# A gated cross-attention kernel on one core: part of the second attention's exponentials moved from ScalarE to VectorE

## Chip, cores and metric

The kernel runs on one core of one Trainium2 chip. The metric is the device time of one execution in microseconds. The engines are called as the profile calls them: PE is TensorE's matmul queue and PEld its weight loads, ACT is ScalarE, DVE is VectorE, POOL is GpSimd, SP is SyncE.

## What is computed

The reference runs two gated blocks over 1024 text rows of width 128 and 6404 context rows of width 96: a first cross-attention (4 heads, top 32 keys) with its own feed-forward part, a low-rank feed-forward block, the second cross-attention, and a mixture of 8 experts. Only the second cross-attention matters here. It has 16 heads of width 8 and a full softmax over all 6404 keys:

```
q = (x @ wq + bq);  k = (y @ wk + bk);  v = (y @ wv + bv)      # 16 heads of 8
scores = einsum('bhqd,bhkd->bhqk', q, k) / sqrt(8)
attn = softmax(scores);  out = einsum('bhqk,bhkd->bhqd', attn, v) @ wo + bo
```

That is 16 x 1024 x 6404 exponentials, 105 million.

## The kernel before

The program is a chain of stages with a barrier after each. The stage of lines 1833 to 1947 is the second attention. Keys lie on the partitions of a score tile and queries on its columns: a tile is 128 keys by 512 queries of one head in f32, which is one PSUM bank. The work goes in 8 passes (`NPASS`): 4 quads of heads by 2 halves of the queries. In a pass the 6404 keys are 50 whole blocks of 128 (`FULL1`) and one last block, whose four heads share one tile on 32 partitions each (`LEFT`). So a pass has 4 x 50 + 1 = 201 tiles (`NTILE`), taken three at a time: 67 units (`NU`).

For each unit PE makes three score matmuls (line 1890, bf16, 52 rows of the contraction, so that two heads lie on the two halves of the array's rows) into three of six PSUM banks, two sets of three in turn. ACT takes the exponential of the three banks in one ACTIVATE of 1536 columns (line 1936) into the ring `ex1` of 12 slots, that is 4 units. PE then sums the values: for a block of keys whose four tiles are done, four f32 matmuls of the weights V (9 columns: 8 values and a one for the sum) into one bank, side by side on four column tiles (line 1905; the trace counts each as two instructions, so a group is 8; line 1909 is the last block's). The exponentials carry no maximum: a bound on the scores, tested in the stage before against `EXP_RANGE`, selects a general path only where it is needed.

The order on PE is written out: `scores(w, u)`, then the group of values that became ready two units back (`ready_at`). Two waits set the pace:

```
pe.wait_ge(S("exped1"), w * NU + u - 1)        # scores(u): the exponentials of unit u-2 are done
act.wait_ge(S("scored1"), w * NU + u + 1)      # ACT: the scores of unit u are done
```

DVE does nothing in a pass but copy the four sums from PSUM at its end (line 1946). POOL clears `o1` once at the start of the stage (line 1862). SP loads the keys and values of quads 2 and 3 as the two buffers come free (line 1866).

Of the kernel before, what the change touches and what calls it, by code (L numbers as in the profile page):

```python
# [25 lines left out]
NG = -(-G // P)  # L26
# [4 lines left out]
H1, DH1 = 16, 8  # L31
VW = DH1 + 1
# [7 lines left out]
NPIECE = G // PIECE  # L40
MASKED = -1.0e30
LOWEST = -3.0e38
EXP_RANGE = 60.0
LN_EPS = 1e-5
ROUND = 12582912.0
assert GP == NG * P
# [46 lines left out]
def program(nc, A, whole):  # L93
# [3 lines left out]
    def S(name):  # L97

        if name not in stage_sems:
            stage_sems[name] = nc.alloc_semaphore(name=f"{name}_{stage[0]}")  # L100
        return stage_sems[name]
# [22 lines left out]
    ps = whole.enter_context(nc.psum_tensor("ps", [P, 8, 512], F32))  # L124
# [1165 lines left out]
    FULL1 = G // P  # L1290
    LEFT = 32
# [4 lines left out]
    K1 = sb(k1s, "K1", [P, 2, 2, GP], BF16)  # L1296
    V1 = sb(k1s, "V1", [P, 2, NG, 4 * VW])

    ROWS1 = ROW1 + LEVELS + 1
# [236 lines left out]
    Q1 = sb(q1s, "Q1", [P, H1, T], BF16)  # L1536
# [71 lines left out]
    with ExitStack() as b7:  # L1608
# [8 lines left out]
        qsel = sb(b7, "qsel", [P, 2, LEVELS, P], BF16)  # L1617
        qline = sb(b7, "qline", [P, 1])
        QP = 3
        SC1 = float(DH1) ** -0.5  # L1620
        with nc.Block() as block:
            @block.sync
            def _(sp):
# [56 lines left out]
            def _(act):  # L1680
# [12 lines left out]
                act.wait_ge(S("bq1s"), 1)  # L1693
                C.activation(qs[:, :], flat(ps[:, 2:4, :]), ACT.Identity, bias=bq1s[:, 0:1], scale=SC1).then_inc(S("q1_sb"), 1)
                act.wait_ge(S("qline_in"), 16)
# [7 lines left out]
            def _(dve):  # L1703
                w = lambda t: t[:, :, :]
                V.tensor_scalar(bq1s[:, :], bq1[:, :], SC1, None, ALU.mult).then_inc(S("bq1s"), 1)
                dchain(V.tensor_scalar(b2r[:, :], b2r[:, :], gt[:, 2:3], None, ALU.mult))
# [24 lines left out]
                dchain(V.reduce_max(bound1[:, :], boundh[:, :], AX.X))  # L1731
                dchain(V.tensor_scalar(bound1[:, :], bound1[:, :], EXP_RANGE, None, ALU.is_gt))
                dchain(V.tensor_copy(general[0:1, 1:2], bound1[:, :]))
# [97 lines left out]


    with ExitStack() as b8:
        NSLOT, NBANK = 12, 3
        ex1 = sb(b8, "ex1", [P, NSLOT, TB])
        NPASS = NQ * NB
        NTILE = 4 * FULL1 + 1
        NU = NTILE // NBANK
        assert NTILE % NBANK == 0 and NSLOT % NBANK == 0


        def last_tile(g):
            return min(4 * g + 3, NTILE - 1)

        def ready_at(g):
            return last_tile(g) // NBANK + 2

        def group_of(tile):

            w, n = divmod(tile, NTILE)  # L1850
            return w * NG + min(n // 4, FULL1)

        def bank(w, n):
            return (w * NTILE + n) % (2 * NBANK)

        def slot(w, n):
            return (w * NTILE + n) % NSLOT

        with nc.Block() as block:
            @block.gpsimd  # L1860
            def _(pool):
                PL.memset(o1[:, :, :], 0.0).then_inc(S("o1_zero"), 1)

            @block.sync
            def _(sp):
                for quad in range(2, NQ):

                    sp.wait_ge(S("scored1"), (quad - 1) * NB * NU)
                    sp.wait_ge(S("summed1"), (quad - 1) * NB * NG)
                    load_quad(sp, quad, S(f"k1_in{quad % 2}"), S(f"v1_in{quad % 2}"))  # L1870

            @block.tensor
            def _(pe):
                def scores(w, u):
                    quad, tb = divmod(w, NB)
                    if quad >= 2 and tb == 0 and u == 0:
                        pe.wait_ge(S(f"k1_in{quad % 2}"), 16 * KIN * (quad // 2))
                    if w * NU + u >= 2:
                        pe.wait_ge(S("exped1"), w * NU + u - 1)
                    for n in range(NBANK * u, NBANK * u + NBANK):  # L1880
                        g = n // 4
                        for hh in ([n % 4] if g < FULL1 else range(4)):
                            rows_ = slice(64 * (hh % 2), 64 * (hh % 2) + ROWS1)
                            if g < FULL1:
                                out, col = ps[:, bank(w, n), :], 0
                                keys = slice(g * P, (g + 1) * P)
                            else:
                                out, col = ps[LEFT * hh:LEFT * (hh + 1), bank(w, n), :], LEFT * hh
                                keys = slice(g * P, g * P + LEFT)
                            last = M.matmul(out, K1[rows_, quad % 2, hh // 2, keys],  # L1890
                                            Q1[rows_, 4 * quad + hh, tb * TB:(tb + 1) * TB], start=True, stop=True,
                                            tile_position=(64 * (hh % 2), col))
                    last.then_inc(S("scored1"), 1)

                def values(w, g):
                    quad = w // NB
                    if g == 0:
                        if quad >= 2 and w % NB == 0:
                            pe.wait_ge(S(f"v1_in{quad % 2}"), 16 * VIN * (quad // 2))
                        if w >= 2:  # L1900
                            pe.wait_ge(S("o1_read"), 4 * (w - 1))
                    for j in range(4):
                        out = ps[32 * j:32 * j + VW, 6 + w % 2, :]
                        if g < FULL1:
                            last = M.matmul(out, V1[:, quad % 2, g, VW * j:VW * j + VW], ex1[:, slot(w, 4 * g + j), :],  # L1905
                                            start=g == 0, stop=False, tile_position=(0, 32 * j))
                        else:
                            left = slice(LEFT * j, LEFT * (j + 1))
                            last = M.matmul(out, V1[left, quad % 2, g, 0:VW], ex1[left, slot(w, NTILE - 1), :],  # L1909
                                            start=False, stop=True, tile_position=(LEFT * j, 32 * j))  # L1910
                    last.then_inc(S("summed1"), 1)

                for w in range(NPASS):
                    for u in range(NU):
                        scores(w, u)
                        for g in range(NG):
                            if w and ready_at(g) == NU + u:
                                values(w - 1, g)
                        for g in range(NG):
                            if ready_at(g) == u:  # L1920
                                values(w, g)
                for g in range(NG):
                    if ready_at(g) >= NU:
                        pe.wait_ge(S("exped1"), (NPASS - 1) * NU + ready_at(g) - 1)
                        values(NPASS - 1, g)

            @block.scalar
            def _(act):
                for w in range(NPASS):
                    for u in range(NU):  # L1930
                        act.wait_ge(S("scored1"), w * NU + u + 1)
                        over = w * NTILE + NBANK * u + NBANK - 1 - NSLOT
                        if over >= 0:
                            act.wait_ge(S("summed1"), group_of(over) + 1)
                        s, b = slot(w, NBANK * u), bank(w, NBANK * u)
                        C.activation(ex1[:, s:s + NBANK, :], ps[:, b:b + NBANK, :], ACT.Exp)\  # L1936
                            .then_inc(S("exped1"), 1)

            @block.vector
            def _(dve):  # L1940
                dve.wait_ge(S("o1_zero"), 1)
                for w in range(NPASS):
                    quad, tb = divmod(w, NB)
                    dve.wait_ge(S("summed1"), (w + 1) * NG)
                    for j in range(4):
                        V.tensor_copy(o1[32 * j:32 * j + VW, quad, tb * TB:(tb + 1) * TB],  # L1946
                                      ps[32 * j:32 * j + VW, 6 + w % 2, :]).then_inc(S("o1_read"), 1)

    q1s.close()
    k1s.close()  # L1950
# [270 lines left out]
```

## Time and profile before

| | us |
|---|---|
| median of 3 runs | 1854.99 |
| lowest, highest | 1853.83, 1858.27 |
| the profiled execution's own time | 1853.31 |
| its span, first to last instruction | 1851.5 |
| the second attention, first score to last copy | 932.2 to 1666.4 |

The rows come from one profiled execution. Times of the timeline and of windows are microseconds from the start of the span. A group of instructions shows its busy time, the mean of one in ns, and the idle time of its engine just before it, with what ended most of it. Instructions of one engine overlap: the mean of one can be longer than the step from one to the next.

### The profile page before, as it was taken

The page shows a single profiled execution, that of the slowest core. Times are in us where ns is not written, and L with a number is a line of the kernel's source. Part 1 is how long each engine was busy: PE and PEld are TensorE (multiplying, and loading weights), DVE is VectorE, ACT ScalarE, POOL GpSimd, SP SyncE. Part 2 cuts the span into 40 slices and gives each one's busy share as a digit, 9 for nine tenths or more (in the row PEclk, how much of TensorE's full clock was granted, in tenths as well). Part 3 has the DMA queues.
Part 4 walks back from the last instruction along what each step waited for, and adds up shares of the span by engine and source line. Part 5 has one row for each costly group of instructions (what it writes and reads, how often), then busy time and mean ns, then how long its engine had stood idle before and what let it go on. Part 6 is the DMA issues. An engine that isn't in the chain of part 4 may idle for free. (4 is left out here: it accounts for less than half of the span.)

```text
span 1851.5 us, 22757 instructions
## 1 busy us (share of the span) xinstructions
PE 1582.9 (85%) x8261; PEld 603.4 (33%) x8261; DVE 854.8 (46%) x2331; ACT 1373.1 (74%) x1441; POOL 169.9 (9%) x154
## 2 busy tenths in 40 slices
PE   6789788898998993776789999999999999985996
PEld 4463354554554552533211111111111111113442
DVE  7768999999999997473400000000000000003223
ACT  5737687888887874313289999999999999982332
POOL 4840211111111101000000000000000000000000
PEclk8869899999999996787689999999999999997998
DMA  3430968979769679350000004000500000003000
GB/s 103 144 117 0 184 150 177 202 155 210 174 151 230 152 179 241 78 152 7 18 1 1 1 1 63 13 1 1 75 1 1 1 1 1 1 1 98 0 1 12
DMA packets 69263, 143.41 MB, mean 77 GB/s; under 512 B 21993, under 2 KB 40642, under 8 KB 68218
## 3 DMA queue, kind: packets, MB, share of 16 engines
q0 software_dynamic: 13616, 75.73, 20.5%
q1 hardware_dynamic: 55098, 65.30, 13.2%
q8 instruction: 69, 1.13, 0.2%
q10 hardware_dynamic: 432, 0.85, 0.1%
q14 instruction: 48, 0.39, 0.1%
HBM read 52.65 MB, written 13.99 MB: 36 GB/s over the span
## 5 line engine op out<-in xcount | busy, mean ns | idle before, releaser
L1936 ACT ACTIVATE ex<-ps 128x1536 f32<-128x1536 f32 x536 | 721.9, 1494 | 6.0 <-PE ps L1890 6.0
L1905 PE MATMUL ps<-ex,V 128*9 128x512 f32 x3200 | 419.8, 597 | 0.5 <-ACT ex L1936 0.4
L850 PE MATMUL ps<-K,qst 128*128 128x512 f32 (+1 forms) x832 | 392.9, 604 | 30.7 <-ACT srow L920 20.7
L1890 PE MATMUL ps<-Q,K 52*128 52x512 bf16 (+1 forms) x1632 | 322.8, 385 | 39.1 <-ACT ex L1936 34.2
L1946 DVE COPY o<-ps 9x512 f32<-9x512 f32 x32 | 22.0, 687 | 714.2 <-PE ps L1909 713.5
L1051 DVE MAX8 cand<-srow 128x8 f32<-128x200 f32 (+1 forms) x1024 | 318.7, 359 | 8.7 <-ACT srow L920 8.6
L1011 DVE SCALAR_TENSOR_TENSOR both<-srow,top,both 128x1536 f32<-128x1536 f32 (+1 forms) x128 | 239.4, 1870 | 21.2 <-ACT both L937 21.0
L920 ACT COPY srow<-ps 128x1024 f32<-128x1024 f32 (+1 forms) x224 | 205.1, 924 | 46.1 <-PE ps L850 45.7
L937 ACT ACTIVATE both<-srow,shift 128x1536 f32<-128x1536 f32 (+1 forms) x128 | 209.4, 1638 | 23.2 <-DMA both<-both 21.8
L1890 PEld LDWEIGHTS ps<-Q,K 52*128 52x128 bf16 (+1 forms) x1632 | 60.7, 94 | 448.1 <-ACT ex L1936 433.1
L850 PEld LDWEIGHTS ps<-K,qst 128*128 128x128 f32 x832 | 150.8, 198 | 166.5 <-issue 116.1
L884 PE MATMUL ps<-v_ring,meanT 128*128 128x128 f32 x716 | 106.1, 293 | 55.3 <-DMA v_ring<-v_rows 49.7
L884 PEld LDWEIGHTS ps<-v_ring,meanT 128*128 128x128 f32 x716 | 95.8, 202 | 97.0 <-issue 48.4
L1103 POOL DMA_DIRECT2D both<-both x92 | 79.1, 860 | 520.1 <-DVE both L1011 486.3
L1905 PEld LDWEIGHTS ps<-ex,V 128*9 128x9 f32 x3200 | 47.7, 89 | 171.2 <-issue 169.4
L2119 ACT ACTIVATE hidm<-ps,b1m 128x512 f32<-128x512 f32 x64 | 43.4, 688 | 75.4 <-PE ps L2072 75.3
L866 PE MATMUL ps<-ident,both 128*128 128x128 f32 (+1 forms) x408 | 64.6, 284 | 17.7 <-DVE both L1071 7.2
L2155 DVE TENSOR_TENSOR hidp<-hidm,ps 128x2048 f32<-128x2048 f32 x16 | 36.6, 2288 | 90.2 <-PE ps L2080 82.3
L866 PEld LDWEIGHTS ps<-ident,both 128*128 128x128 f32 (+1 forms) x408 | 52.0, 146 | 66.4 <-issue 62.2
L2072 PE MATMUL ps<-wT,w1m 128*128 128x512 f32 x128 | 60.2, 615 | 1.4 <-ACT hidm L2119 0.9
L962 ACT COPY meanT<-ps 128x512 f32<-128x512 f32 x96 | 55.9, 585 | 7.1 <-PE ps L866 7.1
L2097 PE MATMUL ps<-hidp,w2m 128*128 128x512 f32 x128 | 58.9, 605 | 0.0
(333 smaller groups left out, 1087.2 us busy)
## 6 DMA issues: line engine op xcount, KB each, us to landing
both<-both POOLq DMA_DIRECT2D x69, 768.0 KB, 8.9
v_ring<-v_rows SPq DMA_DIRECT2D x84, 256.0 KB, 6.3
both<-both POOLq DMA_DIRECT2D x23, 898.0 KB, 13.1
K<-k_parts SPq DMA_DIRECT2D x48, 204.0 KB
k_parts<-kl SPq DMA_DIRECT2D x12, 384.0 KB, 2.6
V<-v_rows SPq DMA_DIRECT2D x4, 900.0 KB, 6.7
v_rows<-v1g SPq DMA_DIRECT2D x12, 288.0 KB, 3.8
srow<-v_rows SPq DMA_DIRECT2D x1, 3200.0 KB, 17.5
```

The source lines that it names most:

```text
L850: last = M.matmul(ps[:, BANK_OF[item] + b, 0:c1 - c0], qst[:, h, :], K0[:, c0:c1], start=True, stop=True)
L866: last = M.transpose(ps[0:w, turn_bank(m), (c % 4) * P:(c % 4 + 1) * P], both[:, mean_of(u), c * P:c * P + w], ident[:, :])
L884: last = M.matmul(ps[:, 7, 0:D], meanT[0:w, m % MSLOTS, (c % 4) * P:(c % 4 + 1) * P], v0_tile(u, c)[0:w, :], start=c == 0, stop=c == NG - 1)
L920: C.copy(srow[:, n % SLOTS, g0:g1], ps[:, b:b + -(-(g1 - g0) // 512), :].rearrange("p a b -> p (a b)")[:, 0:g1 - g0])\
L937: C.activation(both[:, home(n), chunk(c)], srow[:, s, chunk(c)], ACT.Exp, bias=shift[:, s:s + 1])\
L1011: V.scalar_tensor_tensor(both[:, home(n), chunk(c)], srow[:, s, chunk(c)], top40[:, s, TOPK - 1:TOPK], both[:, home(n), chunk(c)], ALU.is_ ...
L1051: last = V.max(eight, srow[:, n % SLOTS, c0:c1])
L1103: PL.dma_start(both[:, mean_of(t), c0:c0 + step], both[:, 0, c0:c0 + step], accum_op=ALU.add).then_inc(S(f"added{c}"), 16)
L1890: last = M.matmul(out, K1[rows_, quad % 2, hh // 2, keys], Q1[rows_, 4 * quad + hh, tb * TB:(tb + 1) * TB], start=True, stop=True, tile_po ...
L1905: last = M.matmul(out, V1[:, quad % 2, g, VW * j:VW * j + VW], ex1[:, slot(w, 4 * g + j), :], start=g == 0, stop=False, tile_position=(0, ...
L1936: C.activation(ex1[:, s:s + NBANK, :], ps[:, b:b + NBANK, :], ACT.Exp)\
L2072: M.matmul(ps[:, f, :], w1[:, e, f * P:(f + 1) * P], wT[:, tb * TB:(tb + 1) * TB], start=True, stop=True).then_inc(S("hidm_ps"), 1)
```

## The change

Three whole key blocks of each pass (47, 48 and 49) leave the units: 4 x 47 + 1 = 189 tiles stay with ACT. Their 12 tiles per pass go to every fifth unit from the seventh on (`OWN` is 6, 11, ..., 61): such a unit has two tiles for ACT and, in its third bank, one of the moved tiles. The number of units stays 67. ACT's instruction for such a unit has 1024 columns, that of the others 1536.

DVE takes the exponential of a moved tile in nine chained instructions on 128 x 512 (`power_of_two`): it reads the bank with a lower bound, rounds the score to a whole number by adding a large constant, forms the fraction, evaluates a polynomial of degree 4 in Horner's form, shifts the rounded number's bits into an exponent, and multiplies. The polynomial is monic, without its leading coefficient `LEAD`, so DVE's exponentials are too large by 1/`LEAD`; ACT gives its own the same factor by the bias `log(1/LEAD)`, a column `common` that POOL sets in the stage's start. The scores are now in units of log 2 (the factor `LOG2E` goes into the scale of the queries), and ACT multiplies by `LN2` in its instruction.

PE sums a block of the moved tiles (`own_values`) when four are done, five units after the last of them (`LATE_AT`: units 26, 46 and 66), from the ring `power` of 8 tiles. Before a unit's scores PE also waits until DVE has read the moved tile of the unit that used the bank (`own_read`). The ring `ex1` is now addressed by units. DVE copies a pass's sums (`read_sums`) ahead of the next pass's tiles. The core of the diff:

```diff
-EXP_RANGE = 60.0
+LOG2E = float(np.log2(np.e))
+LN2 = float(np.log(2.0))
+EXP_RANGE = 60.0 * LOG2E
...
-        SC1 = float(DH1) ** -0.5
+        SC1 = float(DH1) ** -0.5 * LOG2E
...
+        BATCH, BATCHES, EVERY, FIRST_U = 4, 3, 5, 6
+        NOWN = BATCH * BATCHES
+        OWN = [FIRST_U + EVERY * i for i in range(NOWN)]
+        REGULAR = FULL1 - BATCHES
...
+                PL.memset(common[:, :], float(np.log(1.0 / LEAD))).then_inc(S("common_ready"), 1)
...
                     if w * NU + u >= 2:
                         pe.wait_ge(S("exped1"), w * NU + u - 1)
+                        if own_before(w * NU + u - 1):
+                            pe.wait_ge(S("own_read"), own_before(w * NU + u - 1))
...
+                    if u in OWN:
+                        b, j = divmod(OWN.index(u), BATCH)
+                        last = score_tile(w, ps[:, bank(w, u, NBANK - 1), :], 0, REGULAR + b, j)
...
+                def own_values(w, b):
+
+                    quad = w // NB
+                    pe.wait_ge(S("powered"), w * NOWN + BATCH * (b + 1))
+                    for j in range(BATCH):
+                        last = M.matmul(ps[32 * j:32 * j + VW, 6 + w % 2, :], V1[:, quad % 2, REGULAR + b, VW * j:VW * j + VW],
+                                        power[:, (w * NOWN + BATCH * b + j) % (2 * BATCH), :], start=False, stop=False,
+                                        tile_position=(0, 32 * j))
+                    last.then_inc(S("power_used"), 1)
...
+                        if u in LATE_AT:
+                            own_values(w, LATE_AT[u])
...
+                act.wait_ge(S("common_ready"), 1)
                 for w in range(NPASS):
                     for u in range(NU):
                         act.wait_ge(S("scored1"), w * NU + u + 1)
...
-                        C.activation(ex1[:, s:s + NBANK, :], ps[:, b:b + NBANK, :], ACT.Exp)\
+                        s, b, n = slot(w, u, 0), bank(w, u, 0), len(UNITS[u])
+                        C.activation(ex1[:, s:s + n, :], ps[:, b:b + n, :], ACT.Exp, scale=LN2, bias=common[:, 0:1])\
                             .then_inc(S("exped1"), 1)
...
+                def power_of_two(w, i):
+
+                    m = w * NOWN + i
+                    if m:
+                        dve.wait_ge(S("powered"), m)
+                    dve.wait_ge(S("scored1"), w * NU + OWN[i] + 1)
+                    V.tensor_scalar(score[:, :], ps[:, bank(w, OWN[i], NBANK - 1), :], LOW2, None, ALU.max)\
+                        .then_inc(S("own_read"), 1)
+                    dve.wait_ge(S("own_read"), m + 1)
+                    dchain(V.tensor_scalar(whole_[:, :], score[:, :], ROUND2, None, ALU.add))
+                    dchain(V.scalar_tensor_tensor(part[:, :], whole_[:, :], ROUND2, score[:, :], ALU.subtract, ALU.subtract))
+                    dchain(V.scalar_tensor_tensor(poly[:, :], part[:, :], POWER[4], part[:, :], ALU.add, ALU.mult))
+                    for k in (3, 2, 1):
+                        dchain(V.scalar_tensor_tensor(poly[:, :], poly[:, :], POWER[k], part[:, :], ALU.add, ALU.mult))
+                    bits = whole_[:, :].bitcast(I32)
+                    dchain(V.tensor_scalar(bits, bits, 23, None, ALU.logical_shift_left))
+                    if m // BATCH >= 2:
+                        dve.wait_ge(S("power_used"), m // BATCH - 1)
+                    V.scalar_tensor_tensor(power[:, m % (2 * BATCH), :], poly[:, :], POWER[0], whole_[:, :], ALU.add, ALU.mult)\
+                        .then_inc(S("powered"), 1)
```

## Rows read from the trace of the kernel before

**Rows 1.** The page's engine line: busy us, share of the span, instructions.
```profile
PE 1582.9 (85%) x8261; PEld 603.4 (33%) x8261; DVE 854.8 (46%) x2331; ACT 1373.1 (74%) x1441; POOL 169.9 (9%) x154
```

**Rows 2.** Windows: length, then busy PE, PEld, DVE, ACT, POOL; granted clock; DMA share; GB/s.
```profile
942.00:1660.00 718.00, 684.67 (x4839) 107.89 (x4838) 19.24 (x28) 713.54 (x531) 0.00 (x0) 1.00 0.07 11
```

**Rows 3.** The page's groups: busy us, mean ns of one | idle before, releaser.
```profile
L1936 ACT ACTIVATE ex<-ps 128x1536 f32<-128x1536 f32 x536 | 721.9, 1494 | 6.0 <-PE ps L1890 6.0
L1890 PE MATMUL ps<-Q,K 52*128 52x512 bf16 (+1 forms) x1632 | 322.8, 385 | 39.1 <-ACT ex L1936 34.2
L1946 DVE COPY o<-ps 9x512 f32<-9x512 f32 x32 | 22.0, 687 | 714.2 <-PE ps L1909 713.5
```

**Rows 4.** Timeline of ACT: start us, us, engine, line, operation.
```profile
1409.71 31.04 ACT L1936 ACTIVATE ex<-ps 128x1536 f32<-128x1536 f32 x23
```

**Rows 5.** Timeline of PE in the fifth pass.
```profile
1320.82 0.60 PE L1890 MATMUL ps<-Q,K 52*128 52x512 bf16 x3
1321.36 1.04 PE L1905 MATMUL ps<-ex,V 128*9 128x512 f32 x8
1322.34 0.60 PE L1890 MATMUL ps<-Q,K 52*128 52x512 bf16 x3
```

**Rows 6.** Timeline of PE and ACT at a pass's first units.
```profile
1300.88 0.82 PE L1890 MATMUL ps<-Q,K 52*128 52x512 bf16 x6
1301.52 9.51 ACT L1936 ACTIVATE ex<-ps 128x1536 f32<-128x1536 f32 x7 [0.65 <-PE ps L1890]
```

**Rows 7.** Lines and timeline of ACT, from PSUM, no bias column (ns min/median/max).
```profile
L403 ACT ACTIVATE Q<-ps x1: 1023/1023/1023, 16.8 to 16.8; 128x1024 f32<-128x1024 f32 x1
...
407.49 1.93 ACT L920 COPY srow<-ps 128x1024 f32<-128x1024 f32 x2
...
L920 ACT COPY srow<-ps x39: 356/1012/1045, 400.8 to 499.9; 128x1024 f32<-128x1024 f32 x33, 128x260 f32<-128x260 f32 x6
```

**Rows 8.** Lines and timeline of ACT, from PSUM, with a bias column.
```profile
L1699 ACT ACTIVATE Q<-ps,qline x8: 1095/1108/1109, 915.4 to 928.0; 64x1024 bf16<-64x1024 f32 x8
...
917.86 2.11 ACT L1699 ACTIVATE Q<-ps,qline 64x1024 bf16<-64x1024 f32 x2 [1.39 <-PE ps L1670]
...
1706.77 3.00 ACT L2119 ACTIVATE hidm<-ps,b1m 128x512 f32<-128x512 f32 x5
...
L2119 ACT ACTIVATE hidm<-ps,b1m x64: 680/687/712, 1706.8 to 1824.9; 128x512 f32<-128x512 f32 x64
```

**Rows 9.** Timeline and lines of DVE, one and two tensors; POOL beside them.
```profile
14.11 0.23 DVE L489 SCALAR_TENSOR_TENSOR q<-z,q 128x64 f32<-128x64 f32 x1
14.37 0.20 DVE L453 TENSOR_SCALAR q<-q 128x64 f32<-128x64 f32 x1
...
L1507 DVE TENSOR_TENSOR sum_x<-spec_x x2: 682/687/692, 796.0 to 801.6; 128x512 f32<-128x512 f32 x2
...
L1717 DVE CAST ql<-qs x1: 687/687/687, 910.2 to 910.2; 128x1024 bf16<-128x1024 f32 x1
...
L452 DVE TENSOR_TENSOR phase<-rowsT,steps 128x4096 f32<-128x4096 f32 x1 | 4.4, 4416 | 0.0
...
58.97 5.26 DVE L466 SCALAR_TENSOR_TENSOR phaseA<-ub,phaseA 128x4096 f32<-128x4096 f32 x1
...
60.01 4.69 POOL L361 CAST kl<-res 128x512 bf16<-128x512 f32 x1
```

**Rows 10.** Timeline of ACT and POOL at the stage's start and earlier.
```profile
932.23 1.28 ACT L1936 ACT_TABLE_LOAD   x1 [3.07 <-PEq L106]
932.23 3.50 POOL L1862 MEMSET o<- 128x4096 f32 x1 [65.53 <-POOLq L106]
933.52 5.48 ACT L1936 ACTIVATE ex<-ps 128x1536 f32<-128x1536 f32 x4
...
0.27 0.10 POOL L2207 MEMSET const-float32-1.0<- 128x1 f32 x1
...
48.40 1.28 ACT L380 ACT_TABLE_LOAD   x1 [0.34 <-DVE phase L466]
```

More of the change, by code:

```diff
@@ L1833, in program @@
     with ExitStack() as b8:
-        NSLOT, NBANK = 12, 3
-        ex1 = sb(b8, "ex1", [P, NSLOT, TB])
-        NPASS = NQ * NB
[L1837 to L1857, printed above, removed]
+        NBANK, NHELD = 3, 4
+        BATCH, BATCHES, EVERY, FIRST_U = 4, 3, 5, 6
+        NOWN = BATCH * BATCHES
+        OWN = [FIRST_U + EVERY * i for i in range(NOWN)]
+        REGULAR = FULL1 - BATCHES
+        NPASS = NQ * NB
+        NTILE = 4 * REGULAR + 1
+        NSUM = REGULAR + 1
+        ex1 = sb(b8, "ex1", [P, NHELD * NBANK, TB])
+        power = sb(b8, "power", [P, 2 * BATCH, TB])
@@ new lines, in program @@
+        score, whole_, part = (sb(b8, name, [P, TB]) for name in ("score", "whole_part", "part"))
+        poly = score
+        common = sb(b8, "common", [P, 1])
+        UNITS, at = [], 0
+        while at < NTILE:
+            n = NBANK - 1 if len(UNITS) in OWN else NBANK
+            UNITS.append(list(range(at, at + n)))
+            at += n
+        NU = len(UNITS)
+        assert at == NTILE and max(OWN) + EVERY < NU
+        PLACE = {tile: (u, n) for u, tiles in enumerate(UNITS) for n, tile in enumerate(tiles)}
@@ new lines, in program, with block_of @@
+        LATE_AT = {OWN[BATCH * (b + 1) - 1] + EVERY: b for b in range(BATCHES)}
+        LAST_OF = [min(4 * g + 3, NTILE - 1) for g in range(NSUM)]
+        READY_AT = [PLACE[tile][0] + 2 for tile in LAST_OF]
+        LOW2, ROUND2 = -118.0, ROUND + 127.0 + 256.0
+        LEAD = 0.0013276471518916786
+        POWER = tuple(c / -LEAD for c in (1.0000000716546564, -0.6931469670638629, 0.2402211972393386, -0.055507132749627305,
+                                          0.009675541330686871))
+        def block_of(g):
+            return g if g < REGULAR else FULL1
@@ L1859, in program, with own_before, bank, slot @@
+        def own_before(k):
+            w, u = divmod(k, NU)
+            return w * NOWN + sum(1 for o in OWN if o < u)
+        def bank(w, u, n):
+            return (w * NU + u) % 2 * NBANK + n
+        def slot(w, u, n):
+            return (w * NU + u) % NHELD * NBANK + n
         with nc.Block() as block:
@@ L1868, in _ @@
                     sp.wait_ge(S("scored1"), (quad - 1) * NB * NU)
-                    sp.wait_ge(S("summed1"), (quad - 1) * NB * NG)
+                    sp.wait_ge(S("summed1"), (quad - 1) * NB * NSUM)
                     load_quad(sp, quad, S(f"k1_in{quad % 2}"), S(f"v1_in{quad % 2}"))
@@ L1873, in _, with score_tile @@
             def _(pe):
+                def score_tile(w, out, col, g, hh):
+                    quad, tb = divmod(w, NB)
+                    rows_ = slice(64 * (hh % 2), 64 * (hh % 2) + ROWS1)
+                    keys = slice(g * P, (g + 1) * P) if g < FULL1 else slice(g * P, g * P + LEFT)
+                    return M.matmul(out, K1[rows_, quad % 2, hh // 2, keys], Q1[rows_, 4 * quad + hh, tb * TB:(tb + 1) * TB],
+                                    start=True, stop=True, tile_position=(64 * (hh % 2), col))
                 def scores(w, u):
@@ L1879, in scores @@
                         pe.wait_ge(S("exped1"), w * NU + u - 1)
[L1880 to L1892, printed above, removed]
+                        if own_before(w * NU + u - 1):
+                            pe.wait_ge(S("own_read"), own_before(w * NU + u - 1))
+                    for n, tile in enumerate(UNITS[u]):
+                        g, j = block_of(tile // 4), tile % 4
+                        if g < FULL1:
+                            last = score_tile(w, ps[:, bank(w, u, n), :], 0, g, j)
+                        else:
+                            for hh in range(4):
+                                last = score_tile(w, ps[LEFT * hh:LEFT * (hh + 1), bank(w, u, n), :], LEFT * hh, g, hh)
+                    if u in OWN:
+                        b, j = divmod(OWN.index(u), BATCH)
+                        last = score_tile(w, ps[:, bank(w, u, NBANK - 1), :], 0, REGULAR + b, j)
                     last.then_inc(S("scored1"), 1)
@@ L1903, in values @@
                         out = ps[32 * j:32 * j + VW, 6 + w % 2, :]
-                        if g < FULL1:
-                            last = M.matmul(out, V1[:, quad % 2, g, VW * j:VW * j + VW], ex1[:, slot(w, 4 * g + j), :],
+                        if g < REGULAR:
+                            last = M.matmul(out, V1[:, quad % 2, g, VW * j:VW * j + VW], ex1[:, slot(w, *PLACE[4 * g + j]), :],
                                             start=g == 0, stop=False, tile_position=(0, 32 * j))
@@ L1908, in values @@
                             left = slice(LEFT * j, LEFT * (j + 1))
-                            last = M.matmul(out, V1[left, quad % 2, g, 0:VW], ex1[left, slot(w, NTILE - 1), :],
+                            last = M.matmul(out, V1[left, quad % 2, FULL1, 0:VW], ex1[left, slot(w, *PLACE[NTILE - 1]), :],
                                             start=False, stop=True, tile_position=(LEFT * j, 32 * j))
                     last.then_inc(S("summed1"), 1)
+                def own_values(w, b):
[6 more added lines that the diff above has]
+                    last.then_inc(S("power_used"), 1)
                 for w in range(NPASS):
@@ L1915, in _ @@
                         scores(w, u)
-                        for g in range(NG):
-                            if w and ready_at(g) == NU + u:
+                        for g in range(NSUM):
+                            if w and READY_AT[g] == NU + u:
                                 values(w - 1, g)
-                        for g in range(NG):
-                            if ready_at(g) == u:
+                        for g in range(NSUM):
+                            if READY_AT[g] == u:
                                 values(w, g)
-                for g in range(NG):
-                    if ready_at(g) >= NU:
-                        pe.wait_ge(S("exped1"), (NPASS - 1) * NU + ready_at(g) - 1)
+                        if u in LATE_AT:
+                            own_values(w, LATE_AT[u])
+                for g in range(NSUM):
+                    if READY_AT[g] >= NU:
+                        pe.wait_ge(S("exped1"), (NPASS - 1) * NU + READY_AT[g] - 1)
                         values(NPASS - 1, g)
@@ L1931, in _ @@
                         act.wait_ge(S("scored1"), w * NU + u + 1)
[L1932 to L1935, printed above, removed]
-                        C.activation(ex1[:, s:s + NBANK, :], ps[:, b:b + NBANK, :], ACT.Exp)\
+                        if w * NU + u >= NHELD:
+                            ow, ou = divmod(w * NU + u - NHELD, NU)
+                            act.wait_ge(S("summed1"), ow * NSUM + UNITS[ou][-1] // 4 + 1)
+                        s, b, n = slot(w, u, 0), bank(w, u, 0), len(UNITS[u])
+                        C.activation(ex1[:, s:s + n, :], ps[:, b:b + n, :], ACT.Exp, scale=LN2, bias=common[:, 0:1])\
                             .then_inc(S("exped1"), 1)
@@ L1940, in _, with read_sums @@
             def _(dve):
-                dve.wait_ge(S("o1_zero"), 1)
-                for w in range(NPASS):
+                def read_sums(w):
                     quad, tb = divmod(w, NB)
-                    dve.wait_ge(S("summed1"), (w + 1) * NG)
+                    dve.wait_ge(S("power_used"), (w + 1) * BATCHES)
+                    dve.wait_ge(S("summed1"), (w + 1) * NSUM)
                     for j in range(4):
@@ L1947, in _ @@
                                       ps[32 * j:32 * j + VW, 6 + w % 2, :]).then_inc(S("o1_read"), 1)
+                def power_of_two(w, i):
[17 more added lines that the diff above has]
+                        .then_inc(S("powered"), 1)
+                dve.wait_ge(S("o1_zero"), 1)
+                for w in range(NPASS):
+                    if w:
+                        read_sums(w - 1)
+                    for i in range(NOWN):
+                        power_of_two(w, i)
+                read_sums(NPASS - 1)
     q1s.close()
```

## The prediction

> **What bounds the kernel now.** I read the page's engine line first: PE is busy for 85% of the span and ACT for 74% [rows 1], so no engine bounds the whole, and the stage has to be read by itself. The second view is the stretch from 942 to 1660 us, the second attention: in 718 us ACT is busy for 713.54, PE for 684.67, DVE for 19.24, and PE's granted clock is 1.00, the upper of its two levels, 2.4 GHz [rows 2]. Then the groups of instructions: 536 ACTIVATEs of line 1936 sat idle for only 6.0 us in all, while PE sat idle 39.1 us in front of its scores, 34.2 of it for those ACTIVATEs, and DVE waited 714 us [rows 3]. So ACT ends last and PE is about 5% behind it: whatever is taken from ACT is paid out only until PE is full.
>
> The pace comes from the timeline. 23 ACTIVATEs take 31.04 us, and the last of them 1.494, so one follows another after (31.04 − 1.494)/22 = 1.343 us [rows 3, 4]; 536 of them are 719.8 us. On PE the three score matmuls of a unit hold the queue for 0.54 us and a group of values for 0.98 [rows 5], so a unit with a group costs 1.51 against ACT's 1.343, and a unit without one 0.54. Per pass PE needs 67 × 0.54 + 51 × 0.98 = 86.2 us, ACT 90.0. From the start of a unit's scores to its ACTIVATE takes 0.64 us where ACT waits [rows 6].
>
> **Part 1: ACT's elements.** 12 units of 67 in each pass go from 1536 to 1024 columns. Two copies of 1024 columns from PSUM take 1.93 us, one lasts 1.012, so their pace is 0.92 [rows 7]; against 1.343 that is 0.42 us less per unit, for 8 × 12 = 96 units −40.6 us.
>
> **Part 2: ACT's bias.** All 536 ACTIVATEs get the column `common` as bias, where line 1936 has none. The trace has both kinds from PSUM at 1024 columns: without a bias column 1.023 us [rows 7], with one 1.108 [rows 8], so 0.085 more. That it isn't hidden under the neighbour is seen from two paces with a bias: two in 2.11 us give 2.11 − 1.108 = 1.00, against 0.92 without; and five of 512 columns in 3.00 us give (3.00 − 0.69)/4 = 0.578 [rows 8], to which 1024 columns at (1.343 − 0.92)/512 each add 0.846: 1.424 for 1536. I take 1.343 + 0.085 = 1.428 for three banks and 1.00 for two. No row shows an Exp from PSUM with a bias, so the ends are 0 (hidden, the first rival) and 0.13: an Exp of 1536 columns lasts 1.494, which is 0.05 more than 1.023 and 512 more columns give, and that much may come on top; I take 0.085, which two rows give independently. Price: 536 × 0.085 = +45.6 us.
>
> The Trainium skill has a rule that speaks against this change ("ScalarE: Activation LUTs", section "What ACT_TABLE_LOAD costs"): each per-partition pointer operand adds about 93 ns to an ACTIVATE, whatever the function, and back-to-back ones overlap by about 93. By its figure the price would be an estimated 49.8 us in place of 45.6. The trace agrees on the price within 10%; on the overlap it differs, since 1.494 less 1.343 is 0.151 here [rows 3, 4], and the measurement decides.
>
> Parts 1 and 2 together: 440 × 1.428 + 96 × 1.00 = 724.3 us, +4.5 against 719.8. The bias costs more than the three key blocks save.
>
> **Part 3: PE between the ACTIVATEs.** Its matmuls stay the same in number (47 + 3 + 1 groups, 201 tiles per pass). But a unit's scores may not start before the ACTIVATE two units earlier has ended, and ACT must have them 0.64 us before its own start. With the new paces PE may be late by 2 × 1.428 − 1.58 − 0.64 = 0.64 us. Around units 26 and 46, where a group of values from DVE's tiles falls on a unit that has none of its own, five units in a row carry a group: PE loses 4 × 0.08, and 1.51 − 1.00 = 0.51 at the short unit, 0.83 in all, and ACT waits about 0.2. With some hundredths at other short units this is 0.4 us per pass: +3.5 us, 0 to 8. The wait for `own_read` that now stands in front of the scores is met long before: the copy ends 0.7 us after the scores, and the unit that needs the bank is two units on.
>
> **Part 4: the nine DVE instructions.** Per tile: one from PSUM (0.69, as the 512-column copies of line 1946 [rows 3]); two on SBUF with a constant, the addition and the shift; six scalar_tensor_tensor. These take 0.23 at 64 columns, and an instruction with two tensors of 512 columns takes 0.687 [rows 9], so 0.69 each. An SBUF instruction with one tensor has 0.20 at 64 and 0.687 at 1024 columns, so some 0.43 at 512 [rows 9]; for the shift of integers no row exists, and it lies between 0.43 and 0.69. The step from one chained instruction to the next costs 14.37 − 14.11 − 0.23, about 0.03 [rows 9]. Sum: 0.69 + 2 × 0.43 + 6 × 0.69 + 9 × 0.03 = 6.0 us, 6.3 with a slow shift. The upper end is a scalar_tensor_tensor that ran for 5.26 us where a two-tensor instruction of its shape took 4.416 [rows 9], a factor of 1.19, while POOL worked beside it [rows 9]: 6.8 to 7.1 us. A period of five units is 4 × 1.428 + 1.00 = 6.71 us. So I cost it at nothing: it lies in DVE's idle 714 us [rows 3], as do the four copies of `read_sums`, which are due four units ahead of the first tile. If that cover goes, PE stands in `own_values` at `powered`, with the next scores queued behind, and ACT behind those.
>
> **Part 5: the first ACTIVATE.** ACT now waits for `common`, which POOL sets behind its memset of `o1`: 932.23 + 3.50 and 0.1 to 0.2 for the small one, 935.9 [rows 10]. The first ACTIVATE started at 933.52, behind a table load of 1.28 that ran from 932.23 [rows 10]. Delay 2.4 us if the load still runs ahead of the wait, 3.7 if behind it. At line 380, where two waits stand ahead of one ACTIVATE, the load came at 48.40, when the awaited work was done [rows 10]; so I take +3.7.
>
> **Sum:** +4.5 + 3.5 + 3.7 = +11.7 us. The profiled execution took 1853.31 us (span 1851.5), which gives 1865.0; the median of the runs, 1854.99, lies 1.7 higher, and I state **1867**.
>
> **Rival 1: the bias is hidden (not slower).** The column could be fetched while the ACTIVATE in front is still at work, which overlaps the next by 0.151 us anyway. Place: the seam between ACTIVATEs. ACT then needs 440 × 1.343 + 96 × 0.92 = 679.2 us, and PE's 8 × 86.2 = 690 would be the bound. Carrying the start rule of part 3 through ten units by hand gives waits of ACT of 0.22 per five units and in all some 4.5 per pass in place of 0.8: 679.2 + 36 = 715 against 719.8 + 6.0, −11, and with part 5 −7: 1848. It decides once the bias costs under 0.04 us each. For it: no row is an Exp from PSUM with a bias. Against it: two separate paces with a bias, Identity and Gelu, which both give 1.42 to 1.43 [rows 8]. Chance 0.13.
>
> **Rival 2: DVE's chain is too long.** If it exceeds 6.7 us, lateness adds up from tile to tile: a pass then takes 11 chains and 12 units, 11c + 17.1 + 0.7 us for a chain of c; for c = 7.0 that is 94.8 × 8 = 758 against 726, +32, and with part 5 1891; for 6.8 about 1873. For it: the factor of 1.19 above. Against it: that one ran beside POOL, which does nothing in this stage [rows 2]. Chance 0.11.
>
> **Rival 3: half of the bias is hidden,** between 0.03 and 0.06 us each: waits and savings nearly cancel, −6 to +2, with part 5 1853 to 1860. Chance 0.10.
>
> The forecast keeps 0.66: 1860 to 1877, from the ends of parts 3 and 5 and a bias of 0.075 to 0.10.
>
> **Numbers.** About 0.3%, 5.6 us, is what a measurement of this kernel can tell from no change: bounds 1849.4 and 1860.6. Faster has most of rival 1, 0.10; the same has rival 3, the rest of rival 1 and the lower edge of the forecast, 0.18; slower 0.72. The range 1848 to 1884 leaves out half of rival 1 and the worse half of rival 2.
>
> **What would show it.** Right: ACTIVATEs of line 1936's successor at about 1.58 us with 23 in some 32 to 33 us, short ones following after 1.00; ACT idle of 8 to 12 us, PE's idle for ACT up from 34 to about 45; nine DVE instructions in 6.0 to 6.3; first ACTIVATE at about 937. Part 2 is wrong if three banks still follow at 1.34; then ACT's idle rises to some 35 us and PE is the bound. Part 4 is wrong if PE waits for DVE's `power`.

## The result, and the profile after

The changed kernel takes 1867.38 us (median of 6 executions) against 1854.99 before; the ratio is 1.0064, 95% interval 1.0045 to 1.0083, so it is slower, by 0.6%. One of its six executions took 5131.85 us; the ratio leaves it out, no profile of it exists, and the median of the other five is 1866.12. The profiled execution has a span of 1866.8 us.

The spans alone mislead a little: the second attention begins at 935.64 us in this profile and at 932.23 before, and in the profiles further down at 929.2 to 942.6, though the kernels differ ahead of it in constants alone. So I compare the stage by itself, from POOL's memset of `o1` to the end of the last copy of the sums: 734.15 us before (932.23 [rows 10] to 1663.54 + 2.84), 746.29 after (935.64 to 1679.09 + 2.84), 12.1 us more.

The page's groups of the changed kernel, which answer to [rows 3] (busy us, mean ns of one | idle before, releaser), and the groups of ACT with the forms kept apart:

```profile
L1982 ACT ACTIVATE ex<-ps,common 128x1536 f32<-128x1536 f32 (+1 forms) x536 | 731.1, 1483 | 7.7 <-PE ps L1905 6.5
L1905 PE MATMUL ps<-Q,K 52*128 52x512 bf16 (+1 forms) x1632 | 322.7, 385 | 51.4 <-ACT ex L1982 45.1
L2002 DVE TENSOR_SCALAR score<-ps 128x512 f32<-128x512 f32 x96 | 66.4, 692 | 105.6 <-PE ps L1905 105.6
...
L1982 ACT ACTIVATE ex<-ps,common 128x1536 f32<-128x1536 f32 x440 | 647.7, 1558 | 7.7 <-PE ps L1905 6.5 <-POOL common L1888 1.2
L1982 ACT ACTIVATE ex<-ps,common 128x1024 f32<-128x1024 f32 x96 | 109.3, 1139 | 0.0
```

ACT exponentiates 96 tiles fewer and is nevertheless busy for 9.2 us more, 731.1 against 721.9. PE waits more for it, 45.1 us against 34.2. DVE's tiles wait for PE 105.6 us in all, so DVE is not what ends last.

The pace stands in ACT's timeline of the changed kernel; the four lines are the same run of ACTIVATEs, cut after its sixth, seventh, eighth and ninth instruction (start us, us):

```profile
1407.13 8.27 ACT L1982 ACTIVATE ex<-ps,common 128x1536 f32<-128x1536 f32 x6
...
1407.13 9.70 ACT L1982 ACTIVATE ex<-ps,common 128x1536 f32<-128x1536 f32 x7
...
1407.13 10.71 ACT L1982 ACTIVATE ex<-ps,common 128x1536 f32<-128x1536 f32 x8
...
1407.13 12.14 ACT L1982 ACTIVATE ex<-ps,common 128x1536 f32<-128x1536 f32 x9
```

The eighth is a short one, of 1024 columns. Long ones end 1.43 us apart (9.70 − 8.27). The short one starts 1.43 after the seventh and lasts 1.14; the ninth ends at 12.14 and lasts 1.56, so it starts 1.01 after the short one. The paces are 1.43 and 1.01 us, against 1.343 for every unit before [rows 4].

One whole pass, from unit 2 to unit 2 of the next, on ACT's timeline, first of the kernel before, then of the changed one:

```profile
1029.15 90.19 ACT L1936 ACTIVATE ex<-ps 128x1536 f32<-128x1536 f32 x67 [0.57 <-PE ps L1890]
1119.91 5.48 ACT L1936 ACTIVATE ex<-ps 128x1536 f32<-128x1536 f32 x4 [0.57 <-PE ps L1890]
```

```profile
1036.02 91.36 ACT L1982 ACTIVATE ex<-ps,common 128x1536 f32<-128x1536 f32 x67 [0.71 <-PE ps L1905]
1128.09 2.97 ACT L1982 ACTIVATE ex<-ps,common 128x1536 f32<-128x1536 f32 x2 [0.71 <-PE ps L1905]
```

A pass takes 92.07 us in place of 90.76, 1.31 more. The paces account for 55 × 1.43 + 12 × 1.01 − 67 × 1.343 = 0.79 of it. The other 0.52 is put down to waiting between ACTIVATEs, by subtraction: most of it is too short to be listed, since one ACTIVATE still counts as busy while the next could start.

One chain of DVE, the stage's windows and the stage's start in the changed kernel (timeline of DVE; windows with the columns of [rows 2]; timeline of POOL and ACT):

```profile
1409.60 0.69 DVE L2002 TENSOR_SCALAR score<-ps 128x512 f32<-128x512 f32 x1 [2.92 <-PE ps L1905]
1410.32 0.43 DVE L2005 TENSOR_SCALAR whole_part<-score 128x512 f32<-128x512 f32 x1
1410.78 0.69 DVE L2006 SCALAR_TENSOR_TENSOR part<-whole_part,score 128x512 f32<-128x512 f32 x1
...
1412.24 2.15 DVE L2009 SCALAR_TENSOR_TENSOR score<-score,part 128x512 f32<-128x512 f32 x3
1414.42 0.43 DVE L2011 TENSOR_SCALAR whole_part<-whole_part 128x512 int32<-128x512 int32 x1
1414.88 0.69 DVE L2014 SCALAR_TENSOR_TENSOR power<-score,whole_part 128x512 f32<-128x512 f32 x1
1416.25 0.69 DVE L2002 TENSOR_SCALAR score<-ps 128x512 f32<-128x512 f32 x1 [0.68 <-PE ps L1905]
```

```profile
942.00:1660.00 718.00, 675.73 (x4759) 105.38 (x4763) 554.40 (x874) 711.46 (x523) 0.00 (x0) 1.00 0.07 11
```

```profile
935.64 3.50 POOL L1887 MEMSET o<- 128x4096 f32 x1 [66.49 <-POOLq L108]
936.77 1.28 ACT L1982 ACT_TABLE_LOAD   x1 [4.20 <-PE ps L1905]
939.09 0.09 POOL L1888 MEMSET common<- 128x1 f32 x1
939.22 5.83 ACT L1982 ACTIVATE ex<-ps,common 128x1536 f32<-128x1536 f32 x4 [1.17 <-POOL common L1888]
```

A chain runs from 1409.60 to 1415.57, 5.97 us, and DVE then waits 0.68 for its next tile. DVE goes from 19 to 554 us busy in the stretch without being waited for. The granted clock is 1.00 as before. The first ACTIVATE comes 3.58 us after the stage's start, against 1.29 before [rows 10].

### The profile page after: what moved, and what is told of

Its sections match the earlier page's. It is cut to its first block and busy times, and to the rows that moved or that the text cites. A ratio compares the mean times of both kernels' runs of the same rounds, so it can differ in the third digit from the quotient of the medians.

```text
span 1866.8 us, 24340 instructions
## 1 busy us (share of the span) xinstructions
PE 1586.0 (85%) x8261; PEld 605.4 (32%) x8261; DVE 1405.2 (75%) x3195; ACT 1382.5 (74%) x1441; POOL 160.8 (9%) x155
## 5 line engine op out<-in xcount | busy, mean ns | idle before, releaser
L1982 ACT ACTIVATE ex<-ps,common 128x1536 f32<-128x1536 f32 (+1 forms) x536 | 731.1, 1483 | 7.7 <-PE ps L1905 6.5
L1938 PE MATMUL ps<-ex,V 128*9 128x512 f32 x3008 | 394.6, 597 | 0.2 <-ACT ex L1982 0.2
L1905 PE MATMUL ps<-Q,K 52*128 52x512 bf16 (+1 forms) x1632 | 322.7, 385 | 51.4 <-ACT ex L1982 45.1
L2009 DVE SCALAR_TENSOR_TENSOR score<-score,part 128x512 f32<-128x512 f32 x288 | 199.4, 692 | 9.8
L2002 DVE TENSOR_SCALAR score<-ps 128x512 f32<-128x512 f32 x96 | 66.4, 692 | 105.6 <-PE ps L1905 105.6
L2006 DVE SCALAR_TENSOR_TENSOR part<-whole_part,score 128x512 f32<-128x512 f32 x96 | 66.5, 693 | 3.3
L2014 DVE SCALAR_TENSOR_TENSOR power<-score,whole_part 128x512 f32<-128x512 f32 x96 | 66.4, 692 | 3.3
```

The costliest lines, as they stand in the source:

```text
L1905: return M.matmul(out, K1[rows_, quad % 2, hh // 2, keys], Q1[rows_, 4 * quad + hh, tb * TB:(tb + 1) * TB], start=True, stop=True, tile_po ...
L1982: C.activation(ex1[:, s:s + n, :], ps[:, b:b + n, :], ACT.Exp, scale=LN2, bias=common[:, 0:1])\
L2009: dchain(V.scalar_tensor_tensor(poly[:, :], poly[:, :], POWER[k], part[:, :], ALU.add, ALU.mult))
```

## The experiments

All times of the stage below are taken as above, from the memset of `o1` (or of the column, where that comes first) to the end of the last copy. Each is of one profiled execution, and how far it varies from one execution to the next was not measured; within an execution the passes after the first agree to 0.1 us in all but the two runs with a longer chain on DVE, so small differences are better read from a pass.

**The bias by itself.** The kernel before, with nothing but a column of zeros as bias:

```diff
-                        C.activation(ex1[:, s:s + NBANK, :], ps[:, b:b + NBANK, :], ACT.Exp)\
+                        C.activation(ex1[:, s:s + NBANK, :], ps[:, b:b + NBANK, :], ACT.Exp, bias=none[:, 0:1])\
```

> The kernel before with one addition: a column of zeros as bias of all 536 ACTIVATEs, set ahead of the memset of o1. DVE does nothing more than before. Theory: 536 x 0.087 us = 46.6 us more, all of it on ACT which is the bound; pace 1.43, time about 1901, ratio 1.025. Rival (the column is read under cover of the ACTIVATE in front): pace 1.343, time 1855, ratio 1.000.

Measured: 1902.17 us, ratio 1.025 (1.0226 to 1.0274); 45.7 us more in the stage, 779.8 in place of 734.2. The page's groups and one pass on ACT's timeline:

```profile
L1939 ACT ACTIVATE ex<-ps,none 128x1536 f32<-128x1536 f32 x536 | 768.5, 1772 | 3.9 <-PE ps L1892 3.9
L1892 PE MATMUL ps<-Q,K 52*128 52x512 bf16 (+1 forms) x1632 | 322.8, 385 | 84.7 <-ACT ex L1939 80.3
```

```profile
1036.38 96.03 ACT L1939 ACTIVATE ex<-ps,none 128x1536 f32<-128x1536 f32 x67 [0.39 <-PE ps L1892]
1132.81 68.83 ACT L1939 ACTIVATE ex<-ps,none 128x1536 f32<-128x1536 f32 x48 [0.39 <-PE ps L1892]
```

A pass is 96.43 us, 1.44 per unit. DVE was as idle as before, and ACT waited for PE no longer than before (3.9 us against 6.0 [rows 3]), so neither DVE's traffic nor the alternation of PE and ACT has a part in this. A pass grows by 96.43 − 90.76 = 5.67 us, 0.085 on every ACTIVATE, all of it on the path. Divided out of the stage, 45.7 / 536, the price is the same, though some 1.1 of the 45.7 us is the first ACTIVATE, which starts 2.43 us after the stage's start here in place of 1.29. The rival, a read under cover, has fallen.

**The change without the bias.** DVE's first instruction has a second step free; adding log2(LEAD) there brings its exponentials to ACT's scale, and ACT needs no bias (the lower bound rises from −118 to −108; this path is taken only where the bound on the scores is within `EXP_RANGE`, 86.6 in these units):

```diff
-                act.wait_ge(S("common_ready"), 1)
...
-                        C.activation(ex1[:, s:s + n, :], ps[:, b:b + n, :], ACT.Exp, scale=LN2, bias=common[:, 0:1])\
+                        C.activation(ex1[:, s:s + n, :], ps[:, b:b + n, :], ACT.Exp, scale=LN2)\
...
-                    V.tensor_scalar(score[:, :], ps[:, bank(w, OWN[i], NBANK - 1), :], LOW2, None, ALU.max)\
+                    V.tensor_scalar(score[:, :], ps[:, bank(w, OWN[i], NBANK - 1), :], LOW2, float(np.log2(LEAD)), ALU.max, ALU.add)\
```

> The changed kernel, but ACT's instruction has no bias column; the factor 1/LEAD is taken out on the other side, by an addition of log2(LEAD) in the free second step of DVE's first instruction. Theory (the bias column costs 0.087 us on every ACTIVATE's pace): paces go back to 1.343 and 0.92 us, ACT's sum falls by 47 us to 679, but PE, with 8 x 86 us, becomes the bound and ACT's waits grow from 8 to some 35 us; the first ACTIVATE comes 1.3 us after the stage's start; time 1843 to 1849, ratio to before 0.993 to 0.997. Rival (ACT is slowed by DVE's traffic beside it, not by its operand): paces stay at 1.43 and 1.01 and the time at 1865 to 1868.

Measured: 1842.15 us, ratio 0.9934 (0.9909 to 0.9959): faster than both kernels. The stage takes 722.8 us, 11.4 less than before and 23.5 less than with the bias. The page's groups, and one pass on ACT's timeline:

```profile
L1980 ACT ACTIVATE ex<-ps 128x1536 f32<-128x1536 f32 (+1 forms) x536 | 698.8, 1380 | 17.6 <-PE ps L1904 9.0
L1904 PE MATMUL ps<-Q,K 52*128 52x512 bf16 (+1 forms) x1632 | 322.9, 385 | 28.0 <-ACT ex L1980 20.5
```

```profile
1030.98 88.40 ACT L1980 ACTIVATE ex<-ps 128x1536 f32<-128x1536 f32 x67 [1.03 <-PE ps L1904]
1120.41 80.10 ACT L1980 ACTIVATE ex<-ps 128x1536 f32<-128x1536 f32 x61 [1.03 <-PE ps L1904]
```

A pass is 89.43 us, while 55 × 1.343 + 12 × 0.92 = 84.9 is what ACT's paces need: 4.5 us per pass, 36 in all, are waits for PE. Of the 40.6 us that the three blocks take from ACT, 11 arrive.

The paces are seen where ACT did not wait; the three lines are the same run of ACTIVATEs, cut after its fifth, sixth and seventh instruction:

```profile
1405.76 6.62 ACT L1980 ACTIVATE ex<-ps 128x1536 f32<-128x1536 f32 x5
...
1405.76 7.96 ACT L1980 ACTIVATE ex<-ps 128x1536 f32<-128x1536 f32 x6
...
1405.76 8.88 ACT L1980 ACTIVATE ex<-ps 128x1536 f32<-128x1536 f32 x7
```

The sixth, a long one, ends 1.34 us after the fifth, the seventh, a short one, 0.92 after that: the paces without a bias, to 0.01. This run keeps the other thing that the change adds to ACT's instruction, the factor `scale`, and DVE's work beside it. Neither costs ACT anything here, so the rival, DVE's traffic, has fallen.

**What holds the kernel without a bias.** Two runs ask whether PE is simply full, or whether PE and ACT wait for each other in turn. The first moves two of the sums on PE:

```diff
-        LATE_AT = {OWN[BATCH * (b + 1) - 1] + EVERY: b for b in range(BATCHES)}
+        LATE_AT = {29: 0, 49: 1, 66: 2}
```

> Run e1_no_bias with the sums of DVE's first two batches moved on PE from units 26 and 46 to units 29 and 49, which carry no sums of their own either, but lie in another place against the short units. Theory (what holds the kernel without a bias is the alternation of PE and ACT over two sets of banks, by the start rule of the prediction): ACT's waits grow by about 8 us, the time by 6 to 10 us over e1_no_bias. Rival (PE is simply full, so the order of its work does not matter): within 2 us of e1_no_bias.

Measured: 1853.94 us, ratio to before 0.9994 (0.9980 to 1.0007). The stage takes 731.3 us, 8.6 more than 722.8. One pass on ACT's timeline, from unit 2 to unit 2 of the next:

```profile
1025.81 39.29 ACT L1980 ACTIVATE ex<-ps 128x1536 f32<-128x1536 f32 x30 [1.03 <-PE ps L1904]
...
1116.31 39.28 ACT L1980 ACTIVATE ex<-ps 128x1536 f32<-128x1536 f32 x30 [1.03 <-PE ps L1904]
```

A pass is 90.50 us, 1.07 more. The work of every engine is the same; in the stage its order alone gives back three quarters of the gain. By the medians of the times it gives back 11.8 us, more than the 6 to 10 expected, and the kernel cannot be told from the one before; its profiled execution, 1846.57 us, was the fastest of the twelve. Either way PE being simply full is out.

The second leaves the sums of DVE's blocks out of PE's queue (and of the output):

```diff
                     pe.wait_ge(S("powered"), w * NOWN + BATCH * (b + 1))
-                    for j in range(BATCH):
-                        last = M.matmul(...
-                    last.then_inc(S("power_used"), 1)
+                    pe.sem_inc(S("power_used"), 1)
```

> Run e1_no_bias, but PE leaves out the sums of DVE's three key blocks, 3 groups of 0.98 us per pass (so these blocks are missing from the output; DVE still computes their exponentials, and PE still waits for them). In e1_no_bias the stage took 722.8 us. Theory (PE and ACT alternate over two sets of banks, and either waits for the other at the short units): the stage gets 9 us shorter, to 714, ACT's waits fall from some 36 to 27 us. Rival A (PE is full and alone sets the end): 8 x 3 x 0.98 = 23.5 us shorter, 699. Rival B (ACT alone sets it): no change.

Measured, one execution of 1834.71 us: the stage takes 713.9 us, 8.9 less, where 23.5 us of matmuls are gone. One pass on ACT's timeline:

```profile
1115.07 87.66 ACT L1975 ACTIVATE ex<-ps 128x1536 f32<-128x1536 f32 x67 [0.66 <-PE ps L1904]
1203.38 7.74 ACT L1975 ACTIVATE ex<-ps 128x1536 f32<-128x1536 f32 x6 [0.66 <-PE ps L1904]
```

A pass is 88.31 us, 3.4 above ACT's 84.9, so some 27 us of waits are left, as expected. Both rivals have fallen: PE's work is on the path, but only in places.

**One such place.** The sums of a pass's last block go from the next pass's unit 1 to its unit 2:

```diff
-                            if w and READY_AT[g] == NU + u:
+                            if w and READY_AT[g] + (g == NSUM - 1) == NU + u:
```

> Run e1_no_bias with the sums of a pass's last block moved on PE from the next pass's unit 1, where they follow another group, to its unit 2, which has none. There ACT waits 1.03 us at each pass's start. Theory: of these some 0.35 us per pass are won, the rest is the score matmuls of the shared tile and one group more: 2 to 3 us in all, the stage at 720. Rival (the wait comes from the four copies of the sums or from the loads): no change.

Measured: 1840.29 us, ratio 0.9928 (0.9907 to 0.9950). The stage takes 720.3 us, 2.5 less than 722.8, as the rule had it; the times alone cannot tell it from the run without a bias. ACT's timeline can: over three ends of passes, where the run without a bias has a wait of 1.03 us each, none is listed. So that wait came from the place of the sums on PE.

```profile
1019.34 190.83 ACT L1980 ACTIVATE ex<-ps 128x1536 f32<-128x1536 f32 x143
```

**The start.** The two memsets of POOL change places in the changed kernel.

> The changed kernel with the two memsets of POOL in the other order, so that the bias column is ready 0.1 us after the stage's start. Theory: the first ACTIVATE comes some 1.3 us after the stage's start in place of 3.6, and the stage is 2 us shorter (744 in place of 746). Rival (TensorE's warming up sets the first units): the first ACTIVATE is earlier, but the stage stays at 746 us.

Timeline of POOL and ACT:

```profile
931.69 0.09 POOL L1887 MEMSET common<- 128x1 f32 x1 [65.51 <-POOLq L108]
931.72 3.50 POOL L1888 MEMSET o<- 128x4096 f32 x1
932.82 1.28 ACT L1982 ACT_TABLE_LOAD   x1 [4.20 <-PE ps L1905]
934.11 2.97 ACT L1982 ACTIVATE ex<-ps,common 128x1536 f32<-128x1536 f32 x2
```

The first ACTIVATE comes 2.4 us after the stage's start in place of 3.58, and the stage takes 744.5 us in place of 746.3 (one execution, 1863.85 us). The saving, 1.8 us, is nearly the one expected; the first ACTIVATE is not at 1.3, because the table load still waits 1.1 us, for PE's first scores. So it accounts for only 1.2 of the 1.8; the other 0.6 falls within the first pass (93.30 us in place of 93.94 from unit 2 to unit 2), and its cause was not looked for.

**DVE's cover.** The third instruction of the chain is done twice, then three times:

```diff
                     dchain(V.scalar_tensor_tensor(part[:, :], whole_[:, :], ROUND2, score[:, :], ALU.subtract, ALU.subtract))
+                    dchain(V.scalar_tensor_tensor(part[:, :], whole_[:, :], ROUND2, score[:, :], ALU.subtract, ALU.subtract))
```

> The changed kernel with the third of DVE's nine instructions done twice, so that a chain takes 6.0 + 0.73 = 6.7 us against a period of five units of 4 x 1.43 + 1.01 = 6.73. Theory (DVE's chain is covered up to that period): 0 to 3 us more than the changed kernel on the same stretch, PE waits for powered at most 2 us in all. Rival (the chain already ends on the path): 11 x 8 x 0.73 = 64 us more.

Measured, one execution: 1870.99 us, the stage 751.1, 4.9 more than the changed kernel. DVE's timeline, the first instruction of three chains in a row:

```profile
1410.84 0.69 DVE L2002 TENSOR_SCALAR score<-ps 128x512 f32<-128x512 f32 x1 [2.92 <-PE ps L1905]
...
1417.57 0.69 DVE L2002 TENSOR_SCALAR score<-ps 128x512 f32<-128x512 f32 x1
...
1424.30 0.69 DVE L2002 TENSOR_SCALAR score<-ps 128x512 f32<-128x512 f32 x1
```

They follow after 6.73 us, which is the period itself, and the second and third do not wait for PE. PE's weight loads now wait for DVE's `power` 13.2 us, in 24 places of 0.55, one for each batch. Most of each wait passes while PE is still at its scores. Its timeline at the first batch of a pass:

```profile
1437.08 0.60 PE L1905 MATMUL ps<-Q,K 52*128 52x512 bf16 x3
1437.79 1.05 PE L1951 MATMUL ps<-power,V 128*9 128x512 f32 x8
```

The sums start 0.71 us after the scores, against 0.53 in the changed kernel, so 0.18 late; 24 times that is an estimated 4.3 of the 4.9 us. So the cover ends a little below 6.73, not at it, and the time lies 2 us above the range expected. That the chain already lay on the path, at 64 us, is excluded.

> The changed kernel with the third of DVE's nine instructions done three times: a chain of 7.4 us, above the period of 6.73. Theory: a pass takes 11 chains and 12 units, 11 x 7.42 + 12 x 1.43 + 0.7 = 99.5 us in place of 92.1, 8 passes 59 us more: about 1926 us, with PE waiting some 60 us for powered. Rival (DVE has slack over the 12 units between a pass's last tile and the next one's first, so that lateness is made up): no change, 1867.

Measured, one execution: 1976.94 us, the stage 846.0, 99.7 more and not 59. No lateness is made up, so the rival falls, but the formula has only three fifths. Timeline of PE and ACT at a batch's sums, and two windows (columns as in [rows 2]):

```profile
986.43 1.04 PE L1951 MATMUL ps<-power,V 128*9 128x512 f32 x8 [2.30 <-DVE power L2016]
987.41 0.60 PE L1905 MATMUL ps<-Q,K 52*128 52x512 bf16 x3
987.95 1.90 PE L1938 MATMUL ps<-ex,V 128*9 128x512 f32 x8
988.05 1.54 ACT L1982 ACTIVATE ex<-ps,common 128x1536 f32<-128x1536 f32 x1 [2.22 <-PE ps L1905]
989.77 1.03 PE L1905 MATMUL ps<-Q,K 52*128 52x512 bf16 x3
```

```profile
975.00:985.00 10.00, 8.08 (x59) 1.36 (x58) 9.52 (x15) 9.46 (x8) 0.00 (x0) 1.00 0.00 0
988.00:991.00 3.00, 3.00 (x16) 0.32 (x19) 2.86 (x5) 1.70 (x2) 0.00 (x0) 0.50 0.00 0
```

PE waits 2.30 us for `power`, to 986.43, and goes back to work; from 988 to 991 us its granted clock is 0.50, the lower of its two levels, 1.2 GHz. The group of sums there takes 1.90 us in place of 1.05 and the next scores 1.03 in place of 0.60, and ACT waits for both. Over 942 to 1780 us the clock is 0.94.

The missing 41 us are 1.7 for each of the 24 batches. Half of them can be put down to the clock, because after two of the waits it did not fall. Timeline of PE and a window at one of these:

```profile
1405.92 1.04 PE L1951 MATMUL ps<-power,V 128*9 128x512 f32 x8 [2.31 <-DVE power L2016]
```

```profile
1405.00:1415.00 10.00, 8.96 (x66) 1.38 (x66) 9.49 (x16) 7.78 (x7) 0.00 (x0) 1.00 0.37 74
```

As such a wait ends DVE starts a chain, and the step to its next one shows what the stretch behind the wait cost. Here, and after the same wait that ends at 1719.89, the step is 7.46 us, as it is within a batch. After the other 14 waits at a pass's first and second batch the clock fell, and the step was 8.41 to 9.97 us, in all 20 us more than 7.46. Some 16 us of the missing 41 lie at the ends of the passes, over which the formula allows 17.9 us from the last chain to the next pass's first and 19.9 to 21.4 are measured. The clock fell there every time, so the trace has no undisturbed one beside it, and the clock's share in these 16 us is not shown. Some 3.5 us is the chain's step, 7.46 in place of 7.42. Why the clock stayed up after two waits of 2.31 us is open.

## Why the prediction was right

The time was stated as 1867 and is 1867.4; the added 11.7 us stand against 12.1 in the stage. The mechanism was right, but the closeness is in part luck: measured, parts 1 and 2 together are 0.79 us per pass, 6.3 in place of 4.5, part 3 is 4.2 in place of 3.5 and part 5 is 2.3 in place of 3.7, so that errors of +1.8, +0.7 and −1.4 nearly cancel. These sum to 12.8, 0.7 more than the stage's 12.1, which is left unexplained. Step by step:

- **What bounds.** ACT did, and still does in the changed kernel: 7.7 us idle in the stage, just under the 8 to 12 stated, and PE's wait for it up to 45.1, as stated.
- **Part 1, the elements.** 1.343 − 0.92 was taken from copies. The changed kernel has 1.43 and 1.01, the same 0.42 apart, and the run without a bias has 1.34 and 0.92 themselves.
- **Part 2, the bias.** 0.085 us was read from two biased shapes of other functions. The changed kernel shows 1.43 and 1.01, 0.087 and 0.09 more, and the run with the bias alone 0.085 from its passes. The rule of the Trainium skill ("ScalarE: Activation LUTs", section "What ACT_TABLE_LOAD costs", 93 ns for each pointer operand) agrees within a tenth with the 0.085 us measured. This one operand decides the sign of the change: with it +12 us, without it −11.
- **Part 3, PE between the ACTIVATEs.** 3.5 us were summed; 0.52 per pass, 4.2 in all, were measured. The same start rule gave the three later runs in advance: +6 to 10 for the moved sums (8.6 in the stage, 11.8 by the medians of the times), −9 for the sums left out (−8.9 in the stage), −2 to −3 for the last block (−2.5 in the stage).
- **Part 4, DVE.** The chain was summed to 6.0 and takes 5.97; the integer shift, for which no row existed, takes 0.43, the lower of its two bounds. The cover of 6.71 was nearly right: the run with one step more puts its end a little below 6.73.
- **Part 5, the first ACTIVATE.** This is the term that was chosen wrongly between its two bounds: 3.7 us were taken and 2.3 came (3.58 − 1.29). The table load did not wait for `common`; it waited for PE's scores, 1.1 us, and ran ahead of the column, so the lower bound of 2.4 was the right one.
- **The rivals.** The first, a hidden bias, would have given 1848; the run without a bias, at 1842, shows that it was priced right up to its start delay, and the run with the bias alone that it does not happen. The second, a chain that is too long, needs more than 6.7 us, and the run at 7.4 shows it as described, but dearer than 11 chains and 12 units, at least half of that by the clock, which the prediction did not count. The third, half a hidden bias, falls with the first.

## What to carry to other kernels

An instruction that is issued hundreds of times on the engine that bounds must be costed with its operands, not its elements alone: here one per-partition column, needed for a constant factor, cost more than the work that was moved away. Look for a place where such a factor is free, as a second step in the other engine's instruction. And where two engines alternate over two sets of buffers, work taken from one arrives only in part, so carry the start rule through the units before choosing an order: the same sums three units later gave back 8.6 of the stage's 11.4 us.

## What the runs showed that was not expected

With the bias alone an ACTIVATE lasts 1.772 us in the mean, against 1.558 for the long ones in the changed kernel, which have a bias and a scale, and 1.494 without one [rows 3], though its pace is 1.44, hardly more than 1.43. So the mean of one instruction is no measure of what it costs; the step from one to the next is. Why it lasts longer there is open.

The price of a late wait can be more than the wait: in the run with two more steps PE's granted clock fell to the lower level after 14 of 16 waits of 2.2 to 2.3 us within a pass, and DVE's chains then came 0.95 to 2.5 us late; after the other two it stayed up, and nothing was lost beyond the wait.
